# First LayerNorm rows of half 1 shared by VectorE and ScalarE, bias by GpSimd, and the order of ScalarE's last LayerNorm rows

## The chip, the cores and the metric

The kernel runs on one core of a Trainium2 chip. The metric is device microseconds of one execution. Engines: PE is TensorE, DVE is VectorE, ACT is ScalarE, POOL is GpSimd, SP is SyncE, which here only issues DMAs.

## What is computed

One block of a vision tower on eight images of 256x256 (fp32). With the helper functions cut away:

```python
h = tok(x)                       # 3-level Haar transform, band weights from dot products, inverse transform
h = h + attn(layernorm(h))
h = h + ffn(layernorm(h))

def attn(x):                     # c = 256 channels, 64 hidden
    delta = softplus(x @ Wdelta + bdelta)
    B_bar = delta * (x @ Wb + bb)
    A_cum = clip(cumsum(delta * -softplus(A), axis=1), -20, 20)
    A_shift = concat([0, A_cum[:-1]])
    hid = exp(A_cum) * cumsum(B_bar * exp(-A_shift), axis=1)
    return hid @ Wc + bc + x @ Wd + bd

def ffn(x):                      # fake quantisation: one scale for all of x, per row for weights
    xq = fake_quant(x, sigmoid(clip_x) * max(abs(x)) / 127)
    h = silu(xq @ wq(w_gate).T) * (xq @ wq(w_up).T)
    hq = fake_quant(h, sigmoid(clip_down) * max(abs(h)) / 127)
    return hq @ wq(w_down).T
```

## The kernel before, in words

The eight images are two halves of four. A half lies as 128 partitions (4 images x 32 strips) of 8 rows with 256 channels each, so `h[:, half, r, :]` is one row per partition. The program is written out by hand: each engine has one queue of instructions in the order of the code, and semaphores tie them together. Nothing reorders them.

The stages: DVE does the Haar transform of half 0 and the levels of half 1's first step, PE transposes the bands and takes the dot products, DVE puts both halves together again (`synthesise_level`). `own_strips` multiplies the dot products with a mask, `strip_mask`, that GpSimd builds at the start. Then for each half: moments (`moments`, bn_stats), `inverse_std` on ACT gives rstd, `centre` on DVE gives nmr = -mean x rstd, and `normalise` (ACT) or `normalise_rows` (DVE) write the normalised row xn = h x rstd + nmr. For the first LayerNorm ACT writes all rows; for half 1 of the second, ACT writes rows 0 to 4 (`LAST_ACT_ROWS = 5`) and DVE 5 to 7.

PE transposes xn (`xn_transposed`, group 1, rows 4 to 7, comes first for half 1), ACT copies that out of PSUM (`xn_out`), PE makes the projections and the direct part of the mix (`mix_direct`), ACT the softplus and `decays`, DVE `step_size`, `log_decay` (a scan), `state_input` and `state` (a scan), which ends with hT. `mix_state` adds on PE, for each of four pairs of rows, first the bias (bc + bd as three bf16 parts by a row of ones, L567, with parts that GpSimd has split) and then hT @ Wc. `add_mix` on DVE adds the result to h and takes the moments of the second LayerNorm.

DVE also finds the maxima of the FFN weights (`weight_maxima`, `weight_scales`) and clamps them (`clamp_weights`), ACT rounds them (`quantise_weights`). `ffn_weights_transposed` on PE transposes 36 tiles of them into four PSUM banks, eight to a bank. For the last four of the 36 it waits until ACT has emptied the first bank, and for the following two matmuls with ones (dn, the scale of the down weights) until the second is empty; `ffn_weights_out` on ACT does that emptying. PE's queue goes on like this:

```python
            ffn_weights_transposed()
            pe.wait_ge(xmax_ready, 1)
            keep_warm(WARM_FFN, own(1, 3))          # 14 matmuls of 512 columns, result unused
            pe.wait_ge(xtop_ready, 1)
            spread(own(1, 2)[:, 0:P], xtop[:, 0:1]).then_inc(xtops_psum, 1)
            keep_warm(WARM_SCALE, own(1, 3))
            xq_transposed(0)
```

xtop is the largest |xn| per partition; spread over all partitions it gives DVE the one scale of the FFN's input (xinv), with which DVE and ACT round xn. `xq_transposed` also waits until all banks of weights are out. Then come the FFN's units (`gate_up`), a second global maximum, the down products and the stores, none of which the change touches. The line numbers that the rows carry: L413 transposes, L418 keep-warm, L541 projections, L557 mix_direct, L573 mix_state, L617 gate and up; L771 bank copies and L787 normalised rows on ACT, L862 its table load for silu; L1020 normalised rows, L1061 clamps, L1067 step_size, L1091 the first step of state, L1102 mix additions, L1108 maxima on DVE.

## Time and profile before

| what | value |
|---|---|
| median of 3 runs | 151.08 us (150.08, 151.08, 154.04) |
| the profiled execution, its own time | 151.07 us |
| its span, first to last instruction | 149.1 us |
| mean granted TensorE clock | 0.936 of 2.4 GHz |
| PE / DVE / ACT / POOL busy | 80% / 83% / 55% / 24% of the span |
| matmuls, DVE, ACT, POOL instructions | 668, 249, 153, 60 |
| chain that ended last, by engine | PE 35%, DVE 29%, ACT 22%, issue 7%, DMA 3% |
| DMA traffic | 8.01 MB, mean 54 GB/s |

Times in the rows are microseconds from the span's start. A row of the timeline joins neighbouring instructions of one line ("x8"), gives the time from the first's start to the last's end, and in brackets how long the engine had been idle before and which instruction ended the wait. [...]

### The profile page before, as it was taken

How to read it: one execution, taken by the hardware profiler on the slowest of the kernel's cores; microseconds unless marked ns; L12 is line 12 of the kernel's file. 1: busy time of each engine (PE TensorE's matmuls, PEld its weight loads, DVE VectorE, ACT ScalarE, POOL GpSimd, SP SyncE). 2: the span in 40 equal slices, each digit the busy share in tenths (PEclk: the TensorE clock that was granted, in tenths of full speed). 3: DMA queues.
4: the chain of work that ended last, by engine and by line, in shares of the span. 5: the costliest groups of instructions: out<-in, count | busy, mean ns of one | idle time of the engine just before them, and what ended most of it. 6: DMA issues, size and time to landing. Idle time of an engine off the chain costs nothing.

```text
span 149.1 us, 1974 instructions
## 1 busy us (share of the span) xinstructions
PE 119.8 (80%) x668; PEld 77.5 (52%) x668; DVE 124.0 (83%) x249; ACT 81.4 (55%) x153; POOL 36.3 (24%) x60
## 2 busy tenths in 40 slices
PE   0759979984978936999999987669999998798710
PEld 0749958972443614854587564235545333564400
DVE  0799998989899849923999798877989898999991
ACT  4004116231694677229961399966999980894000
POOL 6668991000000000000000000003556660005710
PEclk9999999996599998799999999987999999999975
DMA  3999500000000000000000000000000000001276
GB/s 97 388 421 420 228 4 2 0 0 0 0 0 0 7 0 0 0 0 0 0 0 4 0 0 0 0 0 4 0 4 0 0 0 0 4 0 70 85 226 181
DMA packets 2897, 8.01 MB, mean 54 GB/s; under 512 B 453, under 2 KB 709, under 8 KB 2760
## 3 DMA queue, kind: packets, MB, share of 16 engines
q1 hardware_dynamic: 2600, 7.37, 13.5%
q10 hardware_dynamic: 288, 0.52, 0.9%
q8 instruction: 5, 0.08, 0.2%
q14 instruction: 4, 0.03, 0.1%
HBM read 5.79 MB, written 2.10 MB: 53 GB/s over the span
## 4 chain that ended last, share of the span: by engine, by line
PE 35%; DVE 29%; ACT 22%; issue 7%; DMA 3%; POOL 1%; DVEq 0%; ACTq 0%; POOLq 0%
PE bank L557 8%; ACT early L787 7%; PE bank L473 6%; PE bank L413 5%; PE bank L541 4%; DVE middle L1226 4%; PE bank L573 4%; PE bank L443 4%; DVE state_mem L1233 4%; DVE stats L1005 4%; PE bank L617 3%; DVE amax L1199 3%; DVE raw L1258 3%; ACT wqT L771 3%; ACT raw L892 3%
## 5 line engine op out<-in xcount | busy, mean ns | idle before, releaser
L400 POOL TENSOR_TENSOR early<-raw,state_mem 128x512 f32<-128x512 f32 x10 | 12.7, 1272 | 86.9 <-ACT raw L892 86.9
L617 PE MATMUL bank<-state_mem,wqT 128*128 128x512 bf16 x80 | 19.7, 398 | 1.0 <-ACT state_mem L873 0.8
L787 ACT ACTIVATE early<-h,nmr,rstd 128x256 f32<-128x256 f32 x29 | 14.9, 589 | 5.0 <-DVE nmr L1013 5.0
L885 ACT ACTIVATE state_mem<-bank,gscale 128x512 f32<-128x512 f32 x22 | 15.1, 748 | 2.6 <-PE bank L617 2.6
L557 PE MATMUL bank<-mixer_w,early 128*128 128x256 f32 x64 | 15.9, 405 | 0.0
L418 PE MATMUL bank<-restart,ident 128*128 128x512 bf16 x50 | 13.9, 430 | 1.5 <-DVE stats L1005 1.5
L630 PE MATMUL bank<-wqT,middle 128*128 128x256 bf16 (+1 forms) x96 | 12.8, 274 | 2.4 <-DVE middle L1226 2.4
L557 PEld LDWEIGHTS bank<-mixer_w,early 128*128 128x128 f32 x64 | 12.8, 206 | 2.9 <-issue 1.1
L1199 DVE TENSOR_REDUCE amax<-early 128x1 f32<-128x1024 f32 x11 | 13.2, 1212 | 0.5 <-POOL early L400 0.5
L617 PEld LDWEIGHTS bank<-state_mem,wqT 128*128 128x128 bf16 x80 | 7.7, 101 | 10.9 <-issue 1.7
L733 ACT ACTIVATE early<-bank 128x512 f32<-128x512 f32 x8 | 4.7, 598 | 15.6 <-PE bank L413 15.6
L630 PEld LDWEIGHTS bank<-wqT,middle 128*128 128x128 bf16 (+1 forms) x96 | 8.3, 97 | 7.2 <-DVE middle L1226 3.8
L898 ACT ACTIVATE raw<-early,ainv 128x512 int16<-128x512 f32 x14 | 8.7, 708 | 4.8 <-DVE ainv L1222 4.8
L1005 DVE BATCH_NORM_STATS2 stats<-h 128x6 f32<-128x512 f32 x16 | 10.6, 694 | 0.3
L1207 DVE SCALAR_TENSOR_TENSOR early<-bank,gscale,state_mem 128x512 f32<-128x512 f32 x12 | 8.9, 746 | 2.0 <-ACT state_mem L885 1.3
L413 PE MATMUL bank<-ident,early 128*128 128x128 f32 x32 | 6.5, 319 | 4.7 <-ACT early L787 4.6
L418 PEld LDWEIGHTS bank<-restart,ident 128*128 128x128 bf16 x50 | 5.3, 109 | 7.8 <-issue 2.6
L473 PE MATMUL bank<-wT,early 128*128 128x96 f32 x48 | 9.2, 352 | 0.0
L573 PE MATMUL bank<-mixer_w,state_mem 64*64 64x256 f32 x64 | 9.1, 404 | 0.0
L405 POOL TENSOR_TENSOR early<-state_mem,h 128x512 f32<-128x512 f32 x4 | 5.5, 1385 | 14.3 <-DVE state_mem L1233 14.3
L658 PE MATMUL bank<-ident 128*128 128x128 f32 x20 | 4.6, 428 | 4.7 <-DMA early<-in_x 4.7
L473 PEld LDWEIGHTS bank<-wT,early 128*128 128x128 f32 x48 | 8.2, 211 | 0.0
(158 smaller groups left out, 235.7 us busy)
## 6 DMA issues: line engine op xcount, KB each, us to landing
out<-early SPq DMA_DIRECT2D x7, 256.0 KB, 2.7
early<-in_x SPq DMA_DIRECT2D x1, 1024.0 KB, 9.1
wT<-in_dot_weights SPq DMA_DIRECT2D x1, 784.0 KB, 7.0
raw<-in_gate_rows SPq DMA_DIRECT2D x1, 768.0 KB, 9.1
raw<-in_up_rows SPq DMA_DIRECT2D x1, 768.0 KB, 10.5
raw<-in_down_rows SPq DMA_DIRECT2D x1, 768.0 KB, 11.9
early<-in_x ACTq DMA_DIRECT2D x2, 256.0 KB, 4.8
early<-in_x SPq DMA_DIRECT2D x2, 256.0 KB, 4.6
```

Of the source, the lines that this page charges most:

```text
L400: nc.gpsimd.tensor_tensor(act[:, u, :], up_s[:, m % UPS, :], silu[:, u % SIL, :], ALU.mult).then_inc(pool_act_ready, 1)
L413: return nc.tensor.transpose(dst, src, eye)
L418: nc.tensor.matmul(into[:, :], ident16[:, :], restart[:, 0:PAIR // 2].bitcast(bf16), start=True, stop=True)
L473: nc.tensor.matmul(own(half, 0)[:, 0:3 * S], bandT[:, half, 4 * b + r, :], wT1[:, b, :, r::4], start=(m + r == 0), stop=(m == 2 and r == 3 ...
L557: nc.tensor.matmul(own(half, MIX[n])[:, i * C:(i + 1) * C], xnT[:, half, c, (2 * n + i) * P:(2 * n + i + 1) * P], wd_t[:, c, :], start=(i ...
L573: last = nc.tensor.matmul(dst[p, :], hT[p, half, 2 * n + i::R], wc_t[p, :], start=False, stop=True, skip_group_check=True)
L617: last = nc.tensor.matmul(dst[:, :], w, xqT[:, k, c, :], start=(c == 0), stop=(c == CH - 1))
L630: return nc.tensor.matmul(down_bank(n, i)[:, i * C:(i + 1) * C], act_q[rows, unit_of[t, k], q * P:(q + 1) * P], wdT[rows, t, :], start=sta ...
L787: nc.scalar.activation(xn[:, half, r, :], h[:, half, r, :], ACT.Identity, bias=nmr[:, norm, half, r:r + 1], scale=rstd[:, norm, half, r:r ...
L885: nc.scalar.activation(silu[:, u % SIL, :], bank[2 * (u % 3)][:, :], ACT.Silu, scale=gscale[:, 0, t:t + 1]).then_inc(silu_ready, 1)
L1005: last = nc.vector.bn_stats(stats[:, norm, half, 2 * n:2 * n + 2, :].rearrange("p r k -> p (r k)"), h[:, half, 2 * n:2 * n + 2, :].rearran ...
L1199: nc.vector.tensor_reduce(amax[:, m:m + 1], act[:, 2 * m:2 * m + 2, :].rearrange("p a t -> p (a t)"), AX.X, ALU.max, apply_absolute_value= ...
```

## The change

Four things move, all within the stages ahead of the FFN.

1. The mask: GpSimd now makes a 128x32 pattern (`own_strip`, four affine selects instead of twelve over 128x96 and 128x128), and ACT makes the mask of it with three activations.
2. The bias: the split in three bf16 parts on GpSimd and the eight bias matmuls on PE are gone. The two bias rows are loaded to all 128 partitions (256 KB instead of 6 KB), GpSimd adds them, and then adds the sum to h itself, pair by pair, after hT of the half is ready (`add_bias`, L380 in the new file); `add_mix` waits for it (`biased`).
3. The first LayerNorm of half 1: ACT writes rows 0 to 3 and then does `decays(0)`, DVE writes rows 4 to 7 before `log_decay(0)`.
4. The second LayerNorm of half 1: ACT writes its five rows, then loads the silu table, then empties all banks of weights. DVE's maximum of half 0 is cut in two, one half after the row maximum of half 1.

```diff
-            sp_eng.dma_start(bias_rows[:, :], row_params[:, 0:2 * C]).then_inc(bias_in, 16)
+            sp_eng.dma_start(bias_rows[:, :], row_params[0, 0:2 * C].partition_broadcast(P)).then_inc(bias_in, 16)
...
-            seq.link(nc.gpsimd.memset(strip_mask[:, :, :], 0.0))
-            for level, (lo, hi) in enumerate(((0, 3), (3, 6), (6, NW))):
-                for b in range(B):
-                    step = seq.mark(nc.gpsimd.affine_select(
-                        out=strip_mask[:, lo:hi, :], in_=strip_mask[:, lo:hi, :], compare_op=ALU.not_equal,
-                        fill=0.5 ** (level + 1), base=-S * b, pattern=[[0, hi - lo], [-1, S]], channel_multiplier=1))
-                    seq.wait(step)
+            seq.link(nc.gpsimd.memset(own_strip[:, :], 0.0))
+            for b in range(B):
+                step = nc.gpsimd.affine_select(out=own_strip[:, :], in_=own_strip[:, :], compare_op=ALU.not_equal, fill=1.0,
+                                               base=-S * b, pattern=[[-1, S]], channel_multiplier=1)
...
+            def add_bias(half):
+
+                pool.wait_ge(hT_ready, half + 1)
+                for n in range(R // 2):
+                    rows = h[:, half, 2 * n:2 * n + 2, :]
+                    nc.gpsimd.tensor_tensor(rows, rows, bias.unsqueeze(1).to_broadcast([P, 2, C]),
+                                            ALU.add).then_inc(biased, 1)
 
             pool.wait_ge(bias_in, 16)
-            left = bias_rows[:, 0:C]
-            seq.link(nc.gpsimd.tensor_tensor(left, left, bias_rows[:, C:2 * C], ALU.add))
-            for k in range(3):
-                seq.link(nc.gpsimd.tensor_copy(bpart[:, k, :], left))
...
+            pool.wait_ge(hT_ready, 1)
+            bias = bias_rows[:, 0:C]
+            seq.link(nc.gpsimd.tensor_tensor(bias, bias, bias_rows[:, C:2 * C], ALU.add))
+            for half in range(HALVES):
+                pool.wait_ge(xn_ready, half * R + ACT_ROWS[half])
+                if half:
+                    pool.wait_ge(xn_late_ready, R - ACT_ROWS[1])
+                add_bias(half)
...
-                        pe.wait_ge(xn_ready, half * R + r + 1)
+                        if r >= ACT_ROWS[half]:
+                            pe.wait_ge(xn_late_ready, r - ACT_ROWS[half] + 1)
+                        else:
+                            pe.wait_ge(xn_ready, half * R + r + 1)
...
                 for n in banks:
-                    nc.tensor.matmul(own(half, MIX[n])[:, :], ones3[:, :], bias3[:, :, :].rearrange("p a c -> p (a c)"),
-                                     start=False, stop=False, skip_group_check=True)
...
             nc.scalar.preload_act_table_set("natural_log_exp_and_others")
+            sc.wait_ge(own_ready, 1)
+            for level, (lo, hi) in enumerate(((0, 3), (3, 6), (6, NW))):
+                nc.scalar.activation(strip_mask[:, lo:hi, :], own_strip[:, :].unsqueeze(1).to_broadcast([P, hi - lo, S]),
+                                     ACT.Copy, scale=0.5 ** (level + 1)).then_inc(mask_ready, 1)
...
-            normalise(0, 1, range(R // 2))
+            normalise(0, 1, range(ACT_ROWS[1]))
             decays(0)
-            normalise(0, 1, range(R // 2, R))
             xn_out(1)
...
             inverse_std(1, 1)
-            ffn_weights_out(range(3))
             normalise(1, 1, range(LAST_ACT_ROWS))
-            ffn_weights_out(range(3, 5))
             nc.scalar.preload_act_table_set("silu_and_others")
+            ffn_weights_out(range(5))
...
                     dve.wait_ge(mix_done, half * R // 2 + n + 1)
+                    dve.wait_ge(biased, half * R // 2 + n + 1)
...
             step_size(0)
+            centre(0, 1)
+            normalise_rows(0, 1, range(ACT_ROWS[1], R))
             log_decay(0)
-            centre(0, 1)
             state_input(0)
...
-            dve.wait_ge(xn_ready, 3 * R)
-            maximum(0, 0, slice(0, R)).then_inc(xmax_ready, 1)
+            dve.wait_ge(xn_ready, sum(ACT_ROWS) + R)
+            maximum(0, 0, slice(0, R // 2)).then_inc(xmax_ready, 1)
             centre(1, 1)
             normalise_rows(1, 1, range(LAST_ACT_ROWS, R))
-            dve.wait_ge(xn_late_ready, R - LAST_ACT_ROWS)
+            dve.wait_ge(xn_late_ready, R - ACT_ROWS[1] + R - LAST_ACT_ROWS)
             maximum(1, 1, slice(LAST_ACT_ROWS, R)).then_inc(xmax_ready, 1)
+            maximum(0, 4, slice(R // 2, R)).then_inc(xmax_ready, 1)
```

`ACT_ROWS = (R, R // 2)`: 8 rows in half 0, 4 in half 1. Line numbers of the new file differ from the old by 3 to 6.

DVE's queue from step_size(0) to the weight maxima, before (the two STT-like rows on restart are the scans of log_decay and state):

```order
L1067 TENSOR_TENSOR state_mem<-state_mem 128x512
L1081 SCALAR_TENSOR_TENSOR state_mem<-restart,state_mem 128x512
L1085 TENSOR_SCALAR state_mem<-state_mem,acol 128x512
L1013 SCALAR_TENSOR_TENSOR nmr<-stats,rstd 128x8
L1074 SCALAR_TENSOR_TENSOR state_mem<-bank,cols,state_mem 128x512
L1091 TENSOR_TENSOR state_mem<-state_mem 128x512
L1092 SCALAR_TENSOR_TENSOR state_mem<-restart,state_mem 128x512
L1095 TENSOR_TENSOR state_mem<-state_mem 128x512
L1042 TENSOR_REDUCE wabs<-raw 128x6 x2
```

The same place in the changed kernel:

```order
L1064 TENSOR_TENSOR state_mem<-state_mem 128x512
L1010 SCALAR_TENSOR_TENSOR nmr<-stats,rstd 128x8
L1017 TENSOR_SCALAR early<-h,rstd,nmr 128x256 x4
L1078 SCALAR_TENSOR_TENSOR state_mem<-restart,state_mem 128x512
L1082 TENSOR_SCALAR state_mem<-state_mem,acol 128x512
L1071 SCALAR_TENSOR_TENSOR state_mem<-bank,cols,state_mem 128x512
L1088 TENSOR_TENSOR state_mem<-state_mem 128x512
L1089 SCALAR_TENSOR_TENSOR state_mem<-restart,state_mem 128x512
L1092 TENSOR_TENSOR state_mem<-state_mem 128x512
L1039 TENSOR_REDUCE wabs<-raw 128x6 x2
```

nmr moved ahead of the scan, and four normalised rows (L1017) came in behind it.

ACT's queue from the statistics of half 1's second LayerNorm to the FFN, before (wqT<-bank empties the banks of weights):

```order
L780 ACTIVATE var<-stats,eps 128x8
L782 ACTIVATE rstd<-var 128x8
L771 ACTIVATE wqT<-bank 128x1024 x3
L787 ACTIVATE early<-h,nmr,rstd 128x256 x5
L771 ACTIVATE wqT<-bank 128x1024
L771 ACTIVATE wqT<-bank 128x512
L775 ACTIVATE dn_row<-bank 128x256
L862 ACT_TABLE_LOAD
L870 ACTIVATE state_mem<-early,xinv 128x1024
```

The same place in the changed kernel:

```order
L776 ACTIVATE var<-stats,eps 128x8
L778 ACTIVATE rstd<-var 128x8
L783 ACTIVATE early<-h,nmr,rstd 128x256 x5
L857 ACT_TABLE_LOAD
L767 ACTIVATE wqT<-bank 128x1024 x4
L767 ACTIVATE wqT<-bank 128x512
L771 ACTIVATE dn_row<-bank 128x256
L866 ACTIVATE state_mem<-early,xinv 128x1024
```

All bank copies moved behind the five rows and the table load. PE's queue there is the same in both kernels:

```order
L410 MATMUL bank<-ident,raw 128x128 x36
L516 MATMUL bank<-diag,ones 128x128 x2
L415 MATMUL bank<-restart,ident 128x512 x14
L410 MATMUL bank<-ident,xtop 128x128
L415 MATMUL bank<-restart,ident 128x512 x3
L410 MATMUL bank<-ident,state_mem 128x128 x8
```

It stands so in the changed kernel: the 36 weight transposes, dn, the 14 keep-warm matmuls, then the spread of xtop.

## Rows read from the trace of the kernel before

**Rows 1.** Timeline of PE, 55 to 65 us: start us, us, instruction, [idle before].

```profile
56.72 0.33 PE L413 MATMUL bank<-ident,early 128*128 128x128 f32 x1 [3.37 <-ACT early L787]
...
59.24 3.12 PE L557 MATMUL bank<-mixer_w,early 128*128 128x256 f32 x8
...
63.08 1.89 PE L557 MATMUL bank<-mixer_w,early 128*128 128x256 f32 x8
```

**Rows 2.** Timeline of DVE, 50 to 92 us.

```profile
55.68 0.69 DVE L1091 TENSOR_TENSOR state_mem<-state_mem 128x512 f32<-128x512 f32 x1 [2.00 <-ACT state_mem L818]
...
69.38 0.69 DVE L1067 TENSOR_TENSOR state_mem<-state_mem 128x512 f32<-128x512 f32 x1 [5.11 <-ACT state_mem L812]
...
82.70 0.69 DVE L1102 TENSOR_TENSOR h<-bank,h 128x512 f32<-128x512 f32 x1 [0.90 <-PE bank L573]
...
90.70 1.06 DVE L1020 TENSOR_SCALAR early<-h,rstd,nmr 128x256 f32<-128x256 f32 x3
```

**Rows 3.** Chain that ended last, 64 to 82 us: start us, us, what.

```profile
64.97 3.63 PE bank L541 x16
68.60 0.32 PE bank L567
68.92 1.07 PE bank L573 x8
...
74.16 7.10 PE bank L557 x32
```

**Rows 4.** Timeline of all engines, 88 to 102 us.

```profile
88.30 2.29 DVE L1108 TENSOR_REDUCE xmax<-early 128x1 f32<-128x2048 f32 x1
...
88.79 2.83 ACT L771 ACTIVATE wqT<-bank 128x1024 bf16<-128x1024 bf16 x3
...
91.37 3.19 PE L418 MATMUL bank<-restart,ident 128*128 128x512 bf16 x14
91.50 2.56 ACT L787 ACTIVATE early<-h,nmr,rstd 128x256 f32<-128x256 f32 x5
...
95.03 0.32 PE L413 MATMUL bank<-ident,xtop 128*128 128x128 f32 x1 [0.47 <-DVE xtop L1169]
...
95.74 1.28 ACT L862 ACT_TABLE_LOAD   x1
...
98.81 3.16 PE L617 MATMUL bank<-state_mem,wqT 128*128 128x512 bf16 x8 [0.82 <-ACT state_mem L873]
```

**Rows 5.** Timeline of GpSimd, 2 to 24 us.

```profile
2.78 5.01 POOL L366 TENSOR_SCALAR_AFFINE_SELECT strip_mask<-strip_mask 128x96 f32<-128x96 f32 x12
```

**Rows 6.** Chain that ended last, 5 to 11 us.

```profile
5.84 0.43 DVE early L914
...
6.29 1.76 DVE middle L919 x4
8.05 0.34 DVE early L913
...
9.43 1.47 DVE middle L919 x4
```

**Rows 7.** The page, part 2: GB/s that the DMA engines moved, 40 slices.

```profile
GB/s 97 388 421 420 228 4 2 0 0 0 0 0 0 7 0 0 0 0 0 0 0 4 0 0 0 0 0 4 0 4 0 0 0 0 4 0 70 85 226 181
```

**Rows 8.** Timeline of DVE and GpSimd, 133 to 136 us.

```profile
133.05 0.48 DVE L1258 TENSOR_SCALAR raw<-early,ainv 128x512 int16<-128x512 f32 x1
...
134.61 1.27 POOL L405 TENSOR_TENSOR early<-state_mem,h 128x512 f32<-128x512 f32 x1 [12.08 <-DVE state_mem L1233]
...
134.65 1.52 DVE L1258 TENSOR_SCALAR raw<-early,ainv 128x512 int16<-128x512 f32 x1
```

**Rows 9.** Timeline of PE, matmuls of 512 columns at 36 and 102 us.

```profile
36.45 4.45 PE L418 MATMUL bank<-restart,ident 128*128 128x512 bf16 x10 [1.51 <-DVE stats L1005]
...
102.62 4.51 PE L617 MATMUL bank<-state_mem,wqT 128*128 128x512 bf16 x20
```

**Rows 10.** Windows: length, busy (x) of PE, PEld, DVE, ACT, POOL; PEclk, DMA share, GB/s.

```profile
41.00:42.00 1.00, 0.65 (x3) 0.14 (x1) 0.96 (x4) 1.00 (x4) 0.00 (x0) 0.88 0.00 0
```

More of the change, by code:

```diff
@@ L141, in build_tower @@
         acol = sb("acol", [P, 5])
-        bres = state_mem.take([3, 2, C])
-        bpart = state_mem.take([3, 3, C], bf16, 2)
-        bsel = state_mem.take([3, 3, C])
-        state_mem.clear()
         za = state_mem.take([P, HALVES, PAIR])
@@ L303, in build_tower @@
         LAST_ACT_ROWS = 5
+        ACT_ROWS = (R, R // 2)
         POOL_PAIRS = (0, 1, 2, 3)
```

36 lines of the change are left out of this document (12 added, 24 removed).

## The prediction

> **What bounds the kernel now.** I read the page's shares first: PE 80% and DVE 83% busy, so no engine bounds it alone. Then I read the chain that ended last in order of time, to see which engine holds which stretch, and the timeline for the waits beside it.
>
> The chain begins with DVE's first Haar level and is then mostly PE's. The largest hole in PE is in the middle: its queue reaches the transposes of half 1's rows at 56.72 - 3.37 = 53.35 us, and these wait for ScalarE's normalised rows. In that thin stretch PE's granted clock drops to 0.50, and eight mix matmuls take 3.12 us where the same eight take 1.89 us later [rows 1]. DVE pays for it as well: 2.00 us before state(0) and 5.11 us before step_size(1), but only 0.90 us for half 1's first mix result [rows 2]. So when PE comes earlier, DVE becomes the bound from about 58 us on. PE's bias matmuls, 0.32 us each, stand in the chain of today [rows 3].
>
> The tail is the other place to look. After the last moments (88.30) ScalarE empties three banks of transposed weights. That lets PE finish ffn_weights_transposed and run its 14 keep-warm matmuls from 91.37 to 94.56, just before xtop is ready. The spread of xtop starts at 95.03, and ScalarE's table load ends only at 97.02, after xinv is there; the first FFN matmul starts at 98.81 [rows 4]. Behind it the FFN is untouched by the change.
>
> **Early part.** GpSimd's twelve affine selects of the mask (2.78 to 7.79) become four smaller ones, and ScalarE makes the mask, in a stretch in which it idles until 12.1. Beside the selects DVE's first adds take 0.43 us and four downs 1.76; later 0.34 and 1.47 [rows 5, 6]. 4 x 0.09 + 0.29 = 0.65 us can come off the front of the chain if the third and fourth loads are there by 7.4; they were by 8.05 at the latest. Bounds 0 and 0.65; I take 0.6. The split of the bias on GpSimd (10.7 to 22.9) slows DVE too, but PE covers it: nothing. The bias row grows from 6 KB to 256 KB, ahead of the weights on SP's queue. At the 420 GB/s of the neighbouring slices that is 0.6 us later for them; traffic ends in the fifth slice, by 18.6 us [rows 7], and the first of them is needed at 46: nothing.
>
> **Middle.** DVE takes rows 4 to 7: three such rows take 1.06 us, four 1.45 [rows 2]. They stand before log_decay, but ScalarE, with four rows instead of eight and its decays at once after, no longer keeps state(0) waiting 2.00 us. State(0) ends about 0.4 us earlier (-2.0 for the wait, +1.45 for the rows, +0.2 that is still waited), and the weight scales end at about 63.9 instead of 69.38 - 5.11 = 64.27. PE has rows 4 to 7 at 52.9, before it needs them: from 53.35 it does 2 x 0.9 + 2 x 1.85 us at full clock and starts projections(1) at about 58.8 instead of 64.97. sp is then ready at about 63.2, before DVE is. From 69.38 to 82.70 - 0.90 = 81.80 DVE worked without a gap, 12.4 us [rows 2]; from 63.9 that ends at 76.3, where it starts add_mix(1, 0). PE has that result at 58.8 + 3.6 + 4 x 1.07 + 7.1 + 1.1 = 74.9, so it is DVE that decides, and the 8 x 0.32 = 2.6 us of bias matmuls taken off PE buy nothing: even with its share of them (five of the eight stand ahead of that result, 1.6 us) PE would be at most 0.2 us late. Gain so far 82.70 - 76.3 = 6.4 us.
>
> **The port that GpSimd and DVE meet on.** The eight bias additions on GpSimd (128x512, 1.27 us each) now run beside DVE work that decides: four from about 58.9, when hT(0) is ready, to 63.9, and four from 71 to 76.5. While such an addition ran at 134.61, a DVE tensor_scalar took 1.52 us instead of 0.48 [rows 8]: it waited for the addition to end. In the first window DVE does weight_maxima, one input each, then the small tensor_scalars of weight_scales at 62.9, in the middle of the fourth addition: about 1.0 us. In the second it does mix additions (one input in PSUM) and moments, and the three clamps, tensor_scalars of int16: one of them meets an addition, about 1.2 us. The bounds are 0 (the windows miss each other, or these forms do not wait) and 1.27 us each; I take 2.2 together. The sums h + bias are ready before they are needed (the first at 60, the fifth at 72.3). The stats of half 1 are then ready 6.4 - 2.2 = 4.2 us earlier, at 84.1 instead of 88.30. The Trainium skill (SBUF — State Buffer, Who interferes with whom) has this as a rule: a DVE instruction in a two-port mode, tensor_scalar among them, or with two SBUF inputs, excludes a GpSimd instruction for its whole length, and a tensor_reduce never does. The trace agrees for tensor_scalar (1.52 against 0.48 us), and by the rule the sum stays as it is.
>
> **Tail, where the gain goes.** ScalarE now does its five rows first, then the table load, then empties the banks. PE has four banks for 36 weight transposes: it fills them at about 80.6 and waits for ScalarE. In its queue behind that wait stand the last four transposes, the down scale, the 14 keep-warm matmuls, and only then the spread of xtop. From the last moments, with the rows of [rows 4]: half a maximum 1.15, centre 0.2, five rows 2.5, table load 1.3, two banks 1.83, PE's rest 0.75; keep-warm starts 7.7 us after the moments, at 91.8. PE has done nothing for over 9 us, and a shorter pause dropped it to 0.50, the 1.2 GHz level. A dense run of the same matmuls that began at 36.45 in that state took 0.43 us each, and the granted clock rose only between 41 and 42 us (0.88 on average, so at about 41.2), 4.8 us in [rows 9, 10]; at 2.4 GHz they take 3.19 / 14 = 0.228. So eleven slow and three fast: 5.4 us, with bounds 3.2 (all fast) and 6.0 (all slow). The spread starts at 84.1 + 7.7 + 5.4 = 97.2 us, where xtop is ready at about 90 and waits for PE. Before it was 95.03: 2.2 us later. That replaces a hidden keep-warm by one on the path. From the spread to the FFN it was 3.78 us; the table load no longer delays ScalarE's part, so DVE's path of 3.45 decides: 0.3 off.
> The Trainium skill (ScalarE: Activation LUTs, What ACT_TABLE_LOAD costs) has about 2.66 us for a switch of tables with its drain. Here the next instruction began 1.30 us after the load did, so the row decides; by the page the sum would be 153.8.
>
> **Sum** against the profiled execution's own 151.07 (span 149.1 and 2.0 around it; the median of the three is 151.08): -0.6 + 2.2 - 0.3 = +1.3, **152.4 us**.
>
> **Rivals.**
> *A, the forecast*: gain in the middle, given back by port waits and by the keep-warm at 1.2 GHz. 152.4.
> *B, no port waits*: the additions miss the tensor_scalars or POOL is late enough. Speaks for it that only two or three short instructions are exposed; against it the row of 1.52. 152.4 - 2.2 = 150.2.
> *C, the change does what it says*: PE is not held behind the banks, or the keep-warm ends before xtop. Then xinv comes about 7.2 us after the moments, ScalarE is free at 84.1 + 9.7 = 93.8, and its two steps (1.65) let the FFN start at 95.6 instead of 98.81. 151.07 - 3.2 - 0.6 = 147.2, or 145 without port waits. Against it: the order of PE's queue.
> *D, slower*: PE's clock does not come back within the keep-warm. This adds 0.6 us there and one more slow stretch at the start of the FFN; the one there now makes eight matmuls take 3.16 us where 20 of them take 4.51 later, 1.4 us lost [rows 4, 9]. 152.4 + 2.0 = 154.4. It decides over 2% if the early 0.6 is missing too or the port waits reach their bound.
> *E, keep-warm at full clock*: 152.4 - 2.2 = 150.2; nothing speaks for it after 9 us without work.
>
> **Chances.** A 0.55, B 0.16, C 0.10, D 0.14, E 0.05. The range is 149.6 to 154.5: it holds A, B, E and most of D, and leaves C out. A measurement of this kernel can tell about 2% from no change (148.1 to 154.1). Faster by more: C, 0.10. Slower by more: half of D and the upper end of A, 0.15. The rest, 0.75, lies within.
>
> **What would show it.** Right: DVE without the idle 5.11 us and without 0.90 before the mix; projections(1) near 58; one DVE tensor_scalar at about 63 and one clamp around 76 of over 1.3 us; PE idle for over 8 us after the weight transposes; a granted clock of 0.50 when the keep-warm starts; xtop ready some 6 us before its spread. Wrong: PE reaching the spread before DVE has xtop (C), tensor_scalars at their old lengths (B), a moments end later than 86, or slow matmuls in the FFN for longer than the three microseconds of now (D).

## The result, and the profile after

| kernel | median us | span of the profiled execution | clock | ratio to before, 95% interval |
|---|---|---|---|---|
| before, 4 runs | 151.41 | 149.1 | 0.936 | |
| changed, 4 runs | 149.09 | 147.5 | 0.933 | 0.989 (0.985 to 0.994) |

The change gains 1.1%; a second set of six runs gave 0.987 (0.980 to 0.994). Predicted was a loss of 1.3 us, 152.4 us within 149.6 to 154.5; the measured median lies below that range. In the two profiles the miss is 2.9 us of span: -1.6 instead of +1.3. All ratios leave out executions more than 1.5% longer than the fastest of their kernel, while the medians hold all of them, and the profiles of e2, e4, e8 and e12 are of such longer ones.

The page of the changed kernel, its second part (40 slices of 3.7 us, tenths of the busy share, PEclk the granted clock):

```profile
PE   0659989964789999999992006949999998798710
DVE  0699789968999599999999991089989898999991
POOL 6300000000000003920670000003655660005710
PEclk9999999998677999999999855799999999999996
```

The hole of PE in the middle [rows 1] is gone. A new one stands at slices 23 and 24, and the clock falls there and not at the FFN's start. PE's timeline of the changed kernel, from the weight transposes on (start, us, row, idle before):

```profile
76.31 2.04 PE L410 MATMUL bank<-ident,raw 128*128 128x128 bf16 x32
89.26 0.61 PE L410 MATMUL bank<-ident,raw 128*128 128x128 bf16 x4 [10.91 <-ACT wqT L767]
91.67 4.01 PE L415 MATMUL bank<-restart,ident 128*128 128x512 bf16 x13 [0.22 <-issue]
95.52 0.27 PE L410 MATMUL bank<-ident,xtop 128*128 128x128 f32 x1
99.00 1.89 PE L613 MATMUL bank<-state_mem,wqT 128*128 128x512 bf16 x8 [0.56 <-DVE state_mem L1189]
101.17 4.48 PE L613 MATMUL bank<-state_mem,wqT 128*128 128x512 bf16 x19
```

PE waits 10.91 us for ACT's first bank copy, then works off its queue: the last four weight transposes, the two dn matmuls, the 14 keep-warm matmuls and the spread. The spread of xtop starts at 95.52 instead of 95.03 [rows 4]. (The record of the first keep-warm matmul is missing; they begin at about 91.25.) The first eight FFN matmuls take 1.89 us instead of 3.16. The windows of the changed kernel (length, PE busy, PEclk, DMA) give the clock:

```profile
84.00:90.00 6.00, 0.61 (x4) 0.50 0.00 0
92.00:94.00 2.00, 2.00 (x6) 0.56 0.00 0
94.00:96.00 2.00, 2.00 (x11) 1.00 0.00 0
99.00:103.00 4.00, 4.00 (x24) 1.00 0.00 0
```

The granted clock is 0.50 (1.2 GHz) when PE comes out of the hole, back at 1.00 (2.4 GHz) from about 93.8, during the keep-warm, and stays there. In the kernel before, the same views have 1.00 from 84 to 99 us and this for the FFN's first four microseconds:

```profile
99.00:103.00 4.00, 4.00 (x18) 0.57 0.00 2
```

DVE's timeline of the changed kernel, the two places where GpSimd's additions run beside it, and the wait for the spread:

```profile
62.41 1.22 DVE L1045 TENSOR_SCALAR wscale<-wabs 128x6 f32<-128x6 f32 x3
75.67 1.80 DVE L1058 TENSOR_SCALAR raw<-raw 128x1536 bf16<-128x1536 int16 x2
77.39 0.68 DVE L1100 TENSOR_TENSOR h<-bank,h 128x512 f32<-128x512 f32 x1
95.83 0.29 DVE L1171 TENSOR_REDUCE gmax<-bank 128x1 f32<-128x128 f32 x1 [6.71 <-PE bank L410]
```

No idle time stands before half 1's L1064 (64.25 us) or before the mix result L1100 any more [rows 2]; DVE ran through to the last moments, which end at 82.87 instead of 88.30.

### The profile page after: what moved, and what is told of

It reads as the page before. It is cut to its first block, busy times and chain, and to the rows that moved or that the text cites. A ratio compares the mean times of both kernels' runs of the same rounds, so it can differ in the third digit from the quotient of the medians.

```text
span 147.5 us, 1944 instructions
## 1 busy us (share of the span) xinstructions
PE 112.1 (76%) x655; PEld 74.6 (51%) x660; DVE 123.3 (84%) x254; ACT 80.1 (54%) x152; POOL 32.6 (22%) x46
## 4 chain that ended last, share of the span: by engine, by line
DVE 43%; PE 23%; ACT 17%; issue 10%; DMA 3%; POOL 1%; DVEq 0%; ACTq 0%; POOLq 0%
ACT early L783 7%; PE bank L470 6%; PE bank L410 4%; PE bank L415 4%; DVE middle L1226 4%; PE bank L440 4%; DVE state_mem L1233 4%; DVE wabs L1039 3%; DVE amax L1199 3%; DVE raw L1258 3%; DMA early<-in_x 3%; ACT raw L888 3%; ACT state_mem L881 2%; PE bank L613 2%; DVE h L1100 2%
## 5 line engine op out<-in xcount | busy, mean ns | idle before, releaser
L397 POOL TENSOR_TENSOR early<-raw,state_mem 128x512 f32<-128x512 f32 x10 | 13.0, 1297 | 31.5 <-ACT raw L888 31.5
L613 PE MATMUL bank<-state_mem,wqT 128*128 128x512 bf16 x78 | 18.2, 379 | 0.8 <-DVE state_mem L1189 0.6
L415 PE MATMUL bank<-restart,ident 128*128 128x512 bf16 x47 | 14.6, 463 | 2.2 <-DVE stats L1002 1.9
L783 ACT ACTIVATE early<-h,nmr,rstd 128x256 f32<-128x256 f32 x25 | 12.8, 587 | 3.8 <-DVE nmr L1010 3.8
L557 PE MATMUL bank<-mixer_w,early 128*128 128x256 f32 x64 | 14.7, 382 | 0.0
L557 PEld LDWEIGHTS bank<-mixer_w,early 128*128 128x128 f32 x64 | 11.8, 190 | 2.6 <-issue 1.1
L386 POOL TENSOR_TENSOR bias_rows<-bias_rows 128x256 f32<-128x256 f32 x1 | 0.7, 728 | 52.6 <-DVE state_mem L1092 52.6
L380 POOL TENSOR_TENSOR h<-h,bias_rows 128x512 f32<-128x512 f32 x8 | 10.1, 1292 | 8.1 <-DVE state_mem L1092 8.0
L410 PE MATMUL bank<-ident,raw 128*128 128x128 bf16 x36 | 2.6, 229 | 10.9 <-ACT wqT L767 10.9
```

The source lines that it names most:

```text
L380: nc.gpsimd.tensor_tensor(rows, rows, bias.unsqueeze(1).to_broadcast([P, 2, C]), ALU.add).then_inc(biased, 1)
L397: nc.gpsimd.tensor_tensor(act[:, u, :], up_s[:, m % UPS, :], silu[:, u % SIL, :], ALU.mult).then_inc(pool_act_ready, 1)
L415: nc.tensor.matmul(into[:, :], ident16[:, :], restart[:, 0:PAIR // 2].bitcast(bf16), start=True, stop=True)
L557: nc.tensor.matmul(own(half, MIX[n])[:, i * C:(i + 1) * C], xnT[:, half, c, (2 * n + i) * P:(2 * n + i + 1) * P], wd_t[:, c, :], start=(i ...
L613: last = nc.tensor.matmul(dst[:, :], w, xqT[:, k, c, :], start=(c == 0), stop=(c == CH - 1))
L783: nc.scalar.activation(xn[:, half, r, :], h[:, half, r, :], ACT.Identity, bias=nmr[:, norm, half, r:r + 1], scale=rstd[:, norm, half, r:r ...
```

## The experiments

Parts are counted as in the section on the change: 1 the mask, 2 the bias, 3 the rows of the first LayerNorm, 4 ACT's order with the cut maximum. All ratios are to the kernel before on the same chip.

### Each part alone

**Part 3 alone**, e6_rows_only:

```diff
+        ACT_ROWS = (R, R // 2)
-            normalise(0, 1, range(R // 2))
+            normalise(0, 1, range(ACT_ROWS[1]))
             decays(0)
-            normalise(0, 1, range(R // 2, R))
...
+            normalise_rows(0, 1, range(ACT_ROWS[1], R))
```

> The kernel before with only part 3: ScalarE writes rows 0 to 3 of half 1's first LayerNorm, VectorE rows 4 to 7 ahead of log_decay; decays come at once after ScalarE's rows. Theory 1 (this part alone takes the hole out of PE's queue, and DVE decides from there): DVE's idle 5.11 us before step_size(1) disappear, half 1's moments end near 82.4 instead of 88.3, and since the keep-warm and the table load keep their old distance to the moments nearly all of it reaches the end: 5.5 us faster than before, 145.4 us. Rival (PE's earlier start is lost at the FFN again): within 2 us of before.

Measured 143.01 us, ratio 0.953 (0.945 to 0.961), span 142.8. Its PE timeline:

```profile
83.55 0.40 PE L414 MATMUL bank<-ident,raw 128*128 128x128 bf16 x4 [1.13 <-ACT wqT L775]
85.07 3.19 PE L419 MATMUL bank<-restart,ident 128*128 128x512 bf16 x14
88.72 0.32 PE L414 MATMUL bank<-ident,xtop 128*128 128x128 f32 x1 [0.47 <-DVE xtop L1173]
92.51 3.30 PE L621 MATMUL bank<-state_mem,wqT 128*128 128x512 bf16 x8 [0.82 <-ACT state_mem L876]
```

The spread comes 6.3 us earlier than before and the span is 6.3 us shorter; between them the lengths are close to those of [rows 4]. By the ratio it is 7.2 us. The middle's forecast (6.4 us) holds, and this one part is worth more than the whole change.

**Part 4 alone**, e7_late_only:

```diff
             inverse_std(1, 1)
-            ffn_weights_out(range(3))
             normalise(1, 1, range(LAST_ACT_ROWS))
-            ffn_weights_out(range(3, 5))
             nc.scalar.preload_act_table_set("silu_and_others")
+            ffn_weights_out(range(5))
```

> The kernel before with only part 4: ScalarE's five rows and the table load ahead of all bank copies, and DVE's maximum cut in two. Theory 1 (the bank copies release PE's keep-warm, which then stands on the path to xinv at the low clock): the spread of xtop starts near 100.3 us instead of 95.0, the FFN starts 5 us later: 156 us. Rival (part 4 brings xtop earlier and with it the FFN): 149 to 151 us.

Measured 156.1 us, ratio 1.037 (1.030 to 1.044). PE waits 5.87 us before its last four transposes, the keep-warm takes 4.84 us (98.02 to 102.86) and the spread starts at 102.70.

**Part 1 alone**, e5_mask_only:

```diff
-                    step = seq.mark(nc.gpsimd.affine_select(
-                        out=strip_mask[:, lo:hi, :], in_=strip_mask[:, lo:hi, :], compare_op=ALU.not_equal,
...
+                nc.scalar.activation(strip_mask[:, lo:hi, :], own_strip[:, :].unsqueeze(1).to_broadcast([P, hi - lo, S]),
+                                     ACT.Copy, scale=0.5 ** (level + 1)).then_inc(mask_ready, 1)
```

> The kernel before with part 1 alone (one strip mask on GpSimd, three copies on ScalarE). Theory of the front: the twelve selects (5.01 us) make VectorE's first operations wait a little and nothing more, the bias split on GpSimd from 10.7 us on stays and still slows VectorE's cascade. Own strips of half 0 at about 18.8 us (19.31 before), time about 0.5 us under the kernel before (150.6 beside 151.1). Rival, the whole early gain of the change comes from the mask: own strips at 17.9 and 149.7 us.

Measured 150.93 beside 151.03 us in ten and 23 runs, ratio 1.000 (0.997 to 1.004). In the profile own strips came at 18.65, near the 18.8 of the first theory. Of its 0.5 us the median shows 0.1, and the interval reaches to 0.5 us.

**Part 2 alone**, e13_bias_only:

```diff
-                    nc.tensor.matmul(own(half, MIX[n])[:, :], ones3[:, :], bias3[:, :, :].rearrange("p a c -> p (a c)"),
-                                     start=False, stop=False, skip_group_check=True)
...
+                    nc.gpsimd.tensor_tensor(rows, rows, bias.unsqueeze(1).to_broadcast([P, 2, C]),
+                                            ALU.add).then_inc(biased, 1)
```

> The kernel before with part 2 alone (split and bias matmuls gone, GpSimd adds the bias). Theory of the port with two signs: VectorE's cascade between 10.7 and 15.2 us, in which it shared the time with six small GpSimd operations, is over some 1.2 us earlier (the 128x256 at 0.42 us instead of 0.61 to 0.83), and in the middle the scales take 1.2 and the clamps 1.8 us instead of 0.3 and 1.0; the scales lie beside the hole of TensorE that is still there, so that 0.8 us come back at most. Time about 150.3 us (before 151.1), own strips of half 0 at about 18.3. Rival, the prediction's step (the split hidden, the waits on the path): own strips at 19.2, time 151.9 to 153.

Measured 149.61 us, ratio 0.995 (0.991 to 0.998); own strips at 18.19. The theory of two signs has its direction, a little more than its size. This profile also showed something that neither theory had, PE's timeline again:

```profile
81.86 1.96 PE L404 MATMUL bank<-ident,raw 128*128 128x128 bf16 x32
88.43 0.61 PE L404 MATMUL bank<-ident,raw 128*128 128x128 bf16 x4 [4.61 <-ACT wqT L758]
90.42 5.45 PE L409 MATMUL bank<-restart,ident 128*128 128x512 bf16 x14
95.70 0.27 PE L404 MATMUL bank<-ident,xtop 128*128 128x128 f32 x1
99.18 1.89 PE L604 MATMUL bank<-state_mem,wqT 128*128 128x512 bf16 x8 [0.56 <-DVE state_mem L1175]
```

With ACT's order untouched, PE idles 3.5 us longer at its wait (4.61 us, 1.13 in e6). The eight bias matmuls that are gone make 2.6 us of that: mix_state(1) takes 3.73 us, where e5 has 5.56 (80.54 to 86.10). The rest fits the port waits, which put off the release; no run has it alone. The clock is at 0.50 after it, and the keep-warm takes 5.45 instead of 3.19 us and delays the spread, for which xtop was ready at 93.55.

The single parts, in us of 151: 0.0, -0.8, -7.2, +5.6; their sum is -2.4, the whole change's two ratios give -1.6 and -2.0.

**The two kernels again**, e4_before_again and e10_after_again (no edit):

> The kernel before, unchanged, for a second profile. The profiled execution of before had a granted clock of 0.50 from 99.3 to 102.7 us, just as the FFN started, and its first eight matmuls took 3.16 us; in the changed kernel's profile the clock stayed at 1.00 there and they took 1.89. Theory 2 (the fall comes or does not come from one execution to the next, and has nothing to do with the change): a second profile of the same kernel may show the eight matmuls at 1.9 us and a span about 1.3 to 1.6 us shorter, near 147.6. Rival (the kernel before always falls there, since its keep-warm is over a microsecond earlier): the clock falls at 99 us again and the span is 149.1 again.

> The changed kernel, unchanged, for more timed executions and a second profile, beside the next kernel on the same chip. Theory 2 (where the clock of TensorE falls is chance from one execution to the next; the work around it is fixed): the median stays at 149.1 us, single executions spread over 148 to 150.5, and the second profile shows the same lengths in the middle and the tail (the tensor_scalar and the clamp that wait, the keep-warm at 4.2 to 4.4 us), with the time of its first FFN matmuls at either 1.9 or 3.2 us. Rival (the changed kernel never falls at the FFN's start, because its keep-warm ends over a microsecond nearer to it): 1.9 us again, as in two of its variants.

Measured 151.1 us, ratio 1.001 (0.996 to 1.006), and 148.51 us, ratio 0.987 (0.980 to 0.994). The changed kernel's profile repeats in the middle and the tail: scales 1.21, clamps 1.79, PE idle 10.91, keep-warm 4.30, first FFN matmuls 1.89 us. Its span is 145.9 us, though, 1.6 less than the first. Most of that lies at PE's four keep-warm matmuls ahead of projections(0). In the first profile:

```profile
43.74 1.91 PE L415 MATMUL bank<-restart,ident 128*128 128x512 bf16 x4
45.58 3.88 PE L541 MATMUL bank<-early,mixer_w 128*64 128x512 f32 x16
```

and in e10:

```profile
42.93 1.03 PE L415 MATMUL bank<-restart,ident 128*128 128x512 bf16 x4
44.34 3.68 PE L541 MATMUL bank<-early,mixer_w 128*64 128x512 f32 x16 [0.39 <-ACT early L793]
```

The granted clock was 0.50 from 43 to 45 us in the first and 1.00 from 43 to 46 in e10. From own strips to mix_direct(0) it took 31.5 us in the first and 30.3 in e10, 1.2 us that are no part of the change: the kernel before has the same four matmuls at 1.03 in its first profile and 1.91 in e4.

The profile of before, taken again, has 1.89 us at the first FFN matmuls this time, with the clock at 1.00 from 88 to 108 us, and from there to its end 48.6 us instead of 50.3. Its span is 151.0, not the 147.6 of the first theory: PE's first transposes start at 12.21 instead of 10.94, the four keep-warm matmuls take 1.91 us, and the eight mix matmuls of [rows 1] take 3.62 instead of 3.12.

### ACT's order, with the rest of the change in place

**e1_weights_first**, the changed kernel with part 4's order undone (the diff of part 4 read backwards; the maximum stays cut):

> The changed kernel with only part 4's order on ScalarE undone: three banks of weights are emptied ahead of the five rows, the other two and the table load come behind them (as in the kernel before); the cut of DVE's maximum stays. Theory 1 (PE's queue: the 14 keep-warm matmuls stand between the weight transposes and the spread of xtop, and only ScalarE's bank copies let PE reach them): PE gets to the keep-warm near 86 us instead of 91, it is over when xtop is ready near 89 to 90, the spread starts there instead of at 95.5, the table load ends near 91.5 and the FFN starts near 93 instead of 99.0: 5 to 6 us less than the changed kernel, about 143.5 us. Rival (the order is what brought the gain, since xtop is ready at 89 thanks to it, and the keep-warm matters little): it loses against the changed kernel, 149.5 us or more.

Measured 142.99 us, ratio 0.954 (0.948 to 0.960): the order costs 5.3 us by the ratios (4.9 with the changed kernel's second ratio). PE's timeline:

```profile
83.00 0.61 PE L410 MATMUL bank<-ident,raw 128*128 128x128 bf16 x4 [6.06 <-ACT wqT L767]
84.98 4.36 PE L415 MATMUL bank<-restart,ident 128*128 128x512 bf16 x14
89.19 0.27 PE L410 MATMUL bank<-ident,xtop 128*128 128x128 f32 x1
92.66 1.89 PE L613 MATMUL bank<-state_mem,wqT 128*128 128x512 bf16 x8 [0.56 <-DVE state_mem L1190]
```

The wait ends 6.3 us earlier than in the changed kernel's first profile, and so do the spread and the span (141.2). Of these, 1.4 us were there before the order matters (the clamps start at 74.28 instead of 75.67). Beside e10, which has not lost them, the spread and the span are 4.7 us earlier.

**e2_no_keepwarm**, the changed kernel without the 14 matmuls ahead of the spread, whose result nothing uses:

```diff
             pe.wait_ge(xmax_ready, 1)
-            keep_warm(WARM_FFN, own(1, 3))
```

> The changed kernel without the 14 keep-warm matmuls ahead of the spread of xtop (their result is used nowhere, so the output stays the same). Theory 1: the spread starts right behind the dn matmuls, near 91.3 instead of 95.5 us, and ScalarE's dn copy, free at 92.7, is no longer waited for by much: the FFN would start near 95.5 instead of 99.0, 3.5 us earlier. Theory of the clock: PE then enters the FFN at a granted clock of 0.50 after 10 us of almost nothing and stays there for some 3 to 5 us, where eight matmuls take 3.2 us instead of 1.9: 1.3 to 2.6 us are lost again. Both together: 1 to 2 us faster than the changed kernel, 147 to 148 us. If the keep-warm were hidden it would be slower than the changed kernel, 150 to 151.

Measured 146.81 us in four runs from 145.02 to 147.73, ratio 0.970 (0.961 to 0.978), 2.9 us under the changed kernel by the ratios:

```profile
90.72 0.42 PE L410 MATMUL bank<-ident,xtop 128*128 128x128 f32 x1
94.72 3.59 PE L613 MATMUL bank<-state_mem,wqT 128*128 128x512 bf16 x8 [0.52 <-DVE state_mem L1188]
```

The spread comes 4.8 us earlier, and the FFN then starts at the low clock (3.59 us for eight). From there to the end of the span it takes 51.0 us, 48.5 in e1. So about half of the order's price comes back when the keep-warm is taken off the path; the low clock at the FFN is what its removal costs.

### The bias and the port

**e3_bias_on_pe**, the changed kernel with part 2 undone (the diff of part 2 read backwards):

> The changed kernel with only part 2 undone: the bias is split on GpSimd at the start and added by eight matmuls on PE, GpSimd adds nothing to h. Theory 1 (the port that GpSimd and DVE meet on costs 0.9 us at weight_scales and 0.8 us at the clamps, and PE's bias matmuls cost nothing since DVE decides there): half 1's moments end 1.7 us earlier, near 81.2, less at most 0.2 for PE, and all behind moves with them: 1.5 us faster than the changed kernel, 147.6 us. Rival (the additions by GpSimd are where the gain of the change came from, 8 x 0.32 = 2.6 us of PE): 1.5 to 2.5 us slower than the changed kernel, 150.6 to 151.6.

Measured 149.07 us, ratio 0.989 (0.984 to 0.993), the same as the changed kernel. Its DVE timeline has the old lengths back:

```profile
61.99 0.31 DVE L1058 TENSOR_SCALAR wscale<-wabs 128x6 f32<-128x6 f32 x3
74.34 1.01 DVE L1071 TENSOR_SCALAR raw<-raw 128x1536 bf16<-128x1536 int16 x2
```

So the port waits cost 0.91 + 0.79 = 1.7 us, as a mechanism shown, and something gives them back. Beside e10, e3's own strips come 1.0 us later (18.65 against 17.63), and then DVE waits 0.28 us for PE's first mix result, whose bias matmuls are back. The moments end within 0.2 us of each other (81.24 and 81.40). So most of it is in the front. DVE's second and third Haar level before, beside GpSimd's split of the bias:

```profile
10.92 0.83 DVE L913 TENSOR_TENSOR early<-middle 128x256 f32<-128x256 f32 x1
11.67 0.61 DVE L914 TENSOR_TENSOR early<-middle 128x256 f32<-128x256 f32 x1
12.32 1.44 DVE L919 TENSOR_TENSOR middle<-early 128x128 f32<-128x128 f32 x4
13.80 0.58 DVE L913 TENSOR_TENSOR early<-middle 128x64 f32<-128x64 f32 x1
```

and in the changed kernel, in which GpSimd rests:

```profile
10.71 0.42 DVE L909 TENSOR_TENSOR early<-middle 128x256 f32<-128x256 f32 x1
11.05 0.42 DVE L910 TENSOR_TENSOR early<-middle 128x256 f32<-128x256 f32 x1
11.50 0.90 DVE L915 TENSOR_TENSOR middle<-early 128x128 f32<-128x128 f32 x4
12.43 0.23 DVE L909 TENSOR_TENSOR early<-middle 128x64 f32<-128x64 f32 x1
```

The additions whose two inputs both lie in SBUF wait for GpSimd. The Trainium skill (SBUF — State Buffer, Who interferes with whom) states that: a DVE instruction with two SBUF inputs contends with a GpSimd instruction that reads SBUF. The trace agrees, 0.61 and 0.83 against 0.42 us; the prediction quoted the rule and used it for the tensor_scalars alone. The mix additions, with one input in PSUM, took 0.67 to 0.68 us beside GpSimd's additions and without them.

**e8_rows_mask_split**, the kernel before with parts 1 and 3 and the cut maximum:

> The kernel before with the mask (part 1), the shared rows (part 3) and the cut maximum, but with the bias on PE and ScalarE's old order of weights and rows: the changed kernel with parts 2 and 4 undone. If the two terms add up (part 4's order costs 6.1 us, the port waits of part 2 cost 1.7 and PE's bias matmuls give at most 0.4 back): 149.1 - 6.1 - 1.3 = 141.7 us, 1.3 less than the variant with part 4 alone undone (142.99). If part 2 costs nothing, as the medians of the third run suggest (149.07 against 149.09): 143.0.

Measured 144.6 us, ratio 0.954 (0.945 to 0.964). The median misses both numbers; the ratio is that of e1, which is the second case, part 2 costing nothing. Neither the missing port waits nor the mask brought anything over e1 and e6 that the ratios show.

**e11_split_later**, the same with the split held back:

```diff
             pool.wait_ge(bias_in, 16)
+            pool.wait_ge(wts_ready, 1)
```

> The kernel before with parts 1 and 3 and the split maximum, bias still by TensorE, ScalarE's order as before, and GpSimd's split of the bias held back until VectorE has made the weights of half 0's bands (about 21 us instead of 10.7). Theory: what slowed the cascade was the split beside it; own strips of half 0 at 17.9 us instead of 19.0, and the split now runs beside the synthesis of half 0, which had 0.6 to 1.3 us to spare before half 1's strips. Logits of half 1 (exp) at 36.3 instead of 37.3; time about 142.5 us (the same kernel with the split early gave 144.6 and its parts 143.0). Rival, the split costs the same wherever it lies beside VectorE: exp at 37.3, time 143.5 or more.

Measured 143.89 us, ratio 0.953 (0.947 to 0.958). Own strips at 17.61, a little before the 17.9 of the theory, but the exponential at 37.78: the rival is right. DVE's timeline:

```profile
21.47 0.72 DVE L994 TENSOR_SCALAR wneg<-wts 128x9 f32<-128x9 f32 x1
22.75 0.66 DVE L1007 SCALAR_TENSOR_TENSOR early<-middle,wts 128x32 f32<-128x32 f32 x1
31.36 1.74 DVE L1013 TENSOR_TENSOR h<-early 128x1024 f32<-128x1024 f32 x1
```

In the changed kernel, where GpSimd rests, these take 0.17, 0.24 and 1.22 us. Moved past one stage, the split slows the next.

**e12_sum_early**, e1 with GpSimd's sum of the two bias rows done at 44 instead of 57.7 us:

```diff
             pool.wait_ge(bias_in, 16)
-            pool.wait_ge(hT_ready, 1)
+            pool.wait_ge(xn_ready, R)
```

> The changed kernel with ScalarE's old order of weights and rows, and GpSimd's sum of the two bias rows (0.73 us) done as soon as half 0's eight rows are normalised (about 43 us) instead of at 57.7. Theory of the port: half 0's four additions then end about 0.8 us earlier, at 62.0 instead of 62.8, so that the three scales of VectorE meet next to nothing of them and take about 0.4 us instead of 1.22; the clamps still take 1.8. Time 0.6 to 0.8 us under that kernel's 143.0, about 142.3. Rival, the scales' 1.2 us don't come from the additions: scales at 1.2 and 143.0.

Measured 142.91 us, ratio 0.948 (0.944 to 0.953). The scales take 0.41 us as foreseen; in the median 0.1 us of the 0.8 is to be seen, by the ratios 0.9, and the two intervals overlap: no difference from e1 is shown. In this profile PE's first twelve transposes took 2.82 us instead of the 1.53 of the changed kernel, and DVE waited 2.07 us for PE before own strips (more on that below).

### The clock before the spread and at the FFN

**e14_warm_between**, e12 with PE's hole filled:

```diff
                     if n == 32:
+                        pe.wait_ge(mix_added, R // 2 + 1)
+                        keep_warm(24, own(1, 2))
                         pe.wait_ge(wqT_ready, 1)
```

> The kernel with the bias sum early (changed kernel, ScalarE's old order, 142.9 us), and 24 more keep-warm matmuls on TensorE in its idle stretch before the last four weight transposes (77.5 to 83.9 us). Theory of the clock: the clock stays at 1.00, the fourteen keep-warm matmuls ahead of the spread take 3.2 us instead of 5.1 and end before the maximum of the rows, the spread comes 0.5 us after xtop instead of 1.8 to 1.9: 1.4 us less, about 141.5 us. If then the clock falls at the FFN's start instead (first eight matmuls 2.9 instead of 1.9 us), the gain is given back: 142.5 to 142.9. Rival, the length of the keep-warm isn't the idle time's doing: 5 us again and 142.9.

Measured 143.07 us, ratio 0.948 (0.942 to 0.954):

```profile
77.91 5.34 PE L415 MATMUL bank<-restart,ident 128*128 128x512 bf16 x24
84.92 3.18 PE L415 MATMUL bank<-restart,ident 128*128 128x512 bf16 x14
88.57 0.32 PE L410 MATMUL bank<-ident,xtop 128*128 128x128 f32 x1 [0.47 <-DVE xtop L1172]
92.37 3.23 PE L615 MATMUL bank<-state_mem,wqT 128*128 128x512 bf16 x8 [0.82 <-ACT state_mem L872]
```

The keep-warm is back at 3.18 us (5.10 in e12) and off the path, so the hole was the cause; and the clock falls at the FFN instead. The second half of the expectation came true: gained and given back.

**e15_between_and_clamps**, e14 with the clamps behind GpSimd's additions:

```diff
-            clamp_weights(1)
-            clamp_weights(2)
             add_mix(1, (0,))
+            clamp_weights(1)
+            clamp_weights(2)
```

> The same, and VectorE's two clamps of the weights moved behind the first addition of half 1, past the end of GpSimd's additions. Theory of the port: the two clamps take 1.0 us instead of 1.77, everything behind them on VectorE is 0.7 to 0.8 us earlier, and the time 0.7 us under the first kernel of this call (about 140.8 if that is 141.5). Rival, they still meet: 1.7 us and no gain.

Measured 141.76 us, ratio 0.938 (0.933 to 0.943). The clamps take 1.01 us at 74.72, just after GpSimd's last addition ended at 74.28. The median fell by 1.3 us, more than the 0.7 expected; the profile has PE's fast front as well, which e14's has not.

**e16_longer_warm**, e11 with 16 instead of 14 keep-warm matmuls ahead of the spread and 9 instead of 3 behind it, and **e17_all_filled**, the same on e15:

```diff
-        WARM_NORM, WARM_PROJECT, WARM_FFN, WARM_DOWN, WARM_SCALE = 10, 4, 14, 16, 3
+        WARM_NORM, WARM_PROJECT, WARM_FFN, WARM_DOWN, WARM_SCALE = 10, 4, 16, 16, 3
...
-            keep_warm(WARM_SCALE, own(1, 3))
+            keep_warm(9, own(1, 3))
```

> The kernel with the split of the bias held back (bias by TensorE, 143.9 us), with 16 instead of 14 keep-warm matmuls ahead of the spread and 9 instead of 3 behind it, so that TensorE is busy up to the FFN's first transposes. Theory: the clock doesn't fall there, the eight transposes take 0.61 us instead of 0.96 and the first eight matmuls 1.9 instead of 2.9: 1.3 us less, about 142.6. Rival, the fall is a matter of chance in either kernel (before, run again, had 1.89 with the old pattern): then the median moves by less than 0.6 us.

> The fastest kernel so far (141.8 us: changed kernel, old order on ScalarE, bias sum early, idle stretch of TensorE filled, clamps behind GpSimd's additions), with 16 instead of 14 keep-warm matmuls ahead of the spread and 9 instead of 3 behind it. Theory of the clock: now neither the keep-warm runs at the low clock (3.6 us for 16) nor the FFN's first eight matmuls (1.9 instead of 3.5 us): 1.3 to 1.6 us less, about 140.4 us. Rival, the longer keep-warm delays the spread or the first transposes by as much: 141.8.

e16: 143.99 us, ratio 0.952 (0.947 to 0.957); e17: 141.11 us, ratio 0.935 (0.929 to 0.940), the fastest of all. In both profiles the clock holds, e17's timeline:

```profile
84.50 3.62 PE L415 MATMUL bank<-restart,ident 128*128 128x512 bf16 x16
88.16 0.32 PE L410 MATMUL bank<-ident,xtop 128*128 128x128 f32 x1
91.95 1.89 PE L615 MATMUL bank<-state_mem,wqT 128*128 128x512 bf16 x8 [0.82 <-ACT state_mem L872]
```

In e16's profile xtop to the FFN's second set of matmuls is 6.2 us (89.71 to 95.88), in e11's 7.2 (88.56 to 95.78). In the medians e17 has 0.65 us of an expected 1.3 to 1.6 over e15, and e16 none over e11. That the filled stretches keep the clock up is shown in the profiles, its worth in the median is not.

## Why the prediction was wrong

Two steps make the miss: the FFN that was put down as untouched (1.8 us), and the length of the keep-warm (1.1 us). The steps in the order of the prediction's stages, each by its own number:

**The middle: right.** PE's hole, DVE as the bound behind it and the 6.4 us hold: e6 alone gives 6.3. In the changed kernel DVE starts add_mix(1, 0) at 77.39; the steps gave 76.3 + 2.2 - 0.6 = 77.9. That these are so close is in part luck: the front was 0.8 us and the port waits 0.5 us better than the steps, and the low clock at 43 us, which no step had, took 1.2 us back. In e10, without it, add_mix(1, 0) starts at 75.94.

**The port: right in kind, 1.7 instead of 2.2 us.** The scales and the clamps waited where they were expected to (62.4 and 75.7 us), and mix additions and moments did not. e3, e12 and e15 each take such a wait away by another edit.

**ACT's order: right.** PE's 10.91 us of idle time, xtop at 88.97 with the spread at 95.52, and 3.5 us from there to the FFN (3.78 - 0.3) are as forecast. The weight banks are full at 78.35 instead of 80.6, which only makes the wait longer. The keep-warm's start (91.25 against 91.2) was met by two misses that cancel. The moments ended 0.6 us ahead of their forecast (82.87 against 84.1 - 0.6), and the keep-warm began 8.4 us behind them instead of 7.7; 0.5 of this is PE's dn stage at the low clock, from whose start (90.27) to the keep-warm it is 1.0 us, where it was 0.5 before (90.85 to 91.37).

**The keep-warm's length: 4.3 instead of 5.4 us.** The step counted the 4.8 us of [rows 9, 10] from the keep-warm's first matmul. But PE had already worked off four transposes and the dn matmuls from 89.26 on, and the clock rose at about 93.8. At 0.43 and 0.228 us each, eight or nine of the fourteen ran at 2.4 GHz, not three. That puts the spread 1.1 us ahead of the forecast (95.52 against 97.2 - 0.6).

**"Behind it the FFN is untouched by the change": wrong, and the largest term.** From the first FFN matmul to the end of the span it was 149.1 - 98.81 = 50.3 us and is 147.5 - 99.00 = 48.5. The 1.8 us lie in its first stretch: eight matmuls in 1.89 instead of 3.16, and the next set starts 2.17 instead of 3.81 us after the first matmul. In the changed kernel the clock is still at 1.00 there. The profiles of all 18 runs sort by what the keep-warm did, with one exception.

Where the keep-warm ran right up to the spread (the changed kernel, e1, e3, e7, e10, e12, e13, e16, e17) the eight matmuls took 1.89 us, nine times of nine. Where it had ended and PE waited 0.47 us for xtop (before, e4, e5, e6, e8, e11, e14, e15) they took 2.87 to 3.55 us seven times and 1.89 once (e4), and without a keep-warm (e2) 3.59. The rest of the span goes with it: from the first FFN matmul to the end it is 48.5 to 48.8 us in the ten profiles with 1.89 and 49.6 to 51.0 in the eight others. So in 15 of the 18 the low clock is paid at one place or at the other, and in three at neither: e16 and e17, whose stretches are filled, and e4. The prediction charged it at the new place without crediting it at the old. Its own [rows 4, 9] had the 1.4 us; it used them in rival D alone, as a loss.

Two things are not shown. In the changed kernel the keep-warm both runs up to the spread and begins at the low clock, and no run has the one without the other; e16 and e17 start theirs at 1.00 and hold the clock, but they also fill the gap behind the spread. And since e4 is the kernel before and did not fall at the FFN, the 1.8 us are those of the two profiles compared; what they are in the medians is open.

Together, 1.1 and 1.8 are the 2.9 us by which the span was missed; between the spread and the FFN nothing was off (3.48 us).

**"The split slows DVE too, but PE covers it: nothing": wrong where PE's first transposes are fast.** PE's first twelve transposes (L413, at 10.9 us) take 2.82 us in ten of the 18 profiles and 1.53 in eight, and the profile of before is one of the ten. With slow transposes own strips came at 18.65 to 19.42 whether the split was there (before, e3, e5, e6, e8) or not (e12, e14, e17, and e16, where it is later); e4, whose transposes began at 12.21, is left out. With fast ones they came at 19.09 with the split (e7, the only such profile) and at 17.57 to 18.19 without it. So the split was a bound just behind PE, and the changed kernel's front is 1.4 us earlier in its profile where the steps had 0.6. By the ratio part 2 alone is worth 0.8 us, port waits and slower keep-warm paid.

**The mask's 0.6 us: in the profiles, not in the median.** Where part 1 and the early split are together (e3, e5, e8) PE's first transposes start at 10.20 to 10.47, without part 1 (before, e6, e7) at 10.94 to 10.97 and in e4 at 12.21. But e5 has 0.1 us in 33 runs, and where the rest goes is open.

**"The bias matmuls taken off PE buy nothing": nearly right in the changed kernel.** With them back (e3) DVE waits 0.28 us for the mix result, where the prediction had at most 0.2. With ACT's old order (e13) taking them off costs: PE idles 4.61 instead of 1.13 us, and the keep-warm takes 5.45 instead of 3.19.

**The rivals.** C (147.2) had PE not held and was wrong; B and E (150.2 each) had one term off, and the truth lay below both because of terms that no case had. All five cases shared the untouched FFN, so the range was too narrow on the fast side.

## What to carry to other kernels

When a change moves a stretch in which the matmul engine idles, charge the low clock at the new place and credit it at the old one, and read whether the engine works right up to the next dense stage. Compare two profiles stage by stage, and take two of each kernel: here two of the same kernel differed by 1.6 us, as much as the whole change gained. Work on GpSimd was not free beside DVE additions with two SBUF inputs (0.42 to 0.83 us) or tensor_scalars (1.01 to 1.80 us); beside it reductions, moments and additions out of PSUM kept their lengths. Time the parts of a change alone: this one was a gain of 7 us with a loss of 5.6 folded into it.

## What the runs showed that was not expected

- PE's first twelve fp32 transposes take 1.53 or 2.82 us, while the clock column reads 1.00 in both. Kernels with the same code up to there had both (1.53 in e1, e11 and e15, 2.82 in e12, e16 and e14), so GpSimd's split alone does not decide it; six of the seven profiles with the early split were slow, four of the eleven others. What decides it stays open; it moves a single profile by up to 1.4 us, as much as most of the parts tested.
- The clock fell to 0.50 at the four keep-warm matmuls ahead of projections(0) in four of the 18 profiles (the changed kernel, e2, e4, e7), which then took 1.91 instead of 1.03 us. No part of the change touches them.
- Three DVE tensor_scalars of six elements each took 0.9 us more beside GpSimd (1.22 instead of 0.31). GpSimd's own lengths vary beside DVE: its three tensor_scalars of 3x256 took 4.42 us in e11, 4.97 before and 5.59 in e6, and one and the same addition of that size 0.72 us before and 1.21 in e5. No run has them beside an idle DVE.
- Filling an idle stretch of PE with unused matmuls kept the clock up, 24 at 77.9 us in e14 and 9 at 88.3 us in e17; from the spread to the FFN e17 took 3.79 us, as e6 did with three.
